# Second norm's variance from ScalarE squares, weight splitting spread over two stages, residual pieces re-timed

## The reference

```python
x = x + xattn(layernorm(x), ctx, ctx)     # per batch [512, 2048]
x = x + ffn(layernorm(x), up, down, perm)
# xattn: t = Wt@v, p = Wp@q, g = Wg@k; att = sum(p*g) per group of 64 rows
#        y = Wz @ (att*t) per group; group norm over the group; y*gn_w + gn_b + v
# ffn:   t = x[:, perm] -> 16 heads of 128 columns
#        gelu(t @ up[h]) @ down[h] per head (128 -> 512 -> 128), then the columns back by unperm
```

## Time and profile before

| | us |
|---|---|
| median of 3 runs | 1635.8 (1634.0 to 1637.0) |
| the profiled execution's own time | 1637.5 |
| its span | 1635.7 |
| TensorE busy | 1536.8 (94%) |
| VectorE busy | 1313.6 (80%) |
| ScalarE busy | 922.3 (56%) |
| GpSimd busy | 820.2 (50%) |

### The profile page before, as it was taken

One profiled execution on the slowest core, in us unless ns is written; L12 is line 12 of the kernel. 1 busy time (PEld: TensorE's weight loads), 2 busy tenths in 40 slices (PEclk: granted clock), 3 DMA queues, 4 the chain that ended last, 5 costly groups with the idle time before them and its releaser, 6 DMA issues.

```text
span 1635.7 us, 19277 instructions
## 1 busy us (share of the span) xinstructions
PE 1536.8 (94%) x6592; PEld 1236.0 (76%) x6592; DVE 1313.6 (80%) x1872; ACT 922.3 (56%) x949; POOL 820.2 (50%) x717
## 2 busy tenths in 40 slices
...
GB/s 316 360 303 353 271 236 132 334 212 249 109 243 252 255 165 155 285 210 249 146 216 276 206 266 99 247 246 263 207 129 258 231 276 136 148 144 305 208 266 203
DMA packets 127024, 374.77 MB, mean 229 GB/s; under 512 B 24528, under 2 KB 32720, under 8 KB 118736
## 3 DMA queue, kind: packets, MB, share of 16 engines
...
## 4 chain that ended last, share of the span: by engine, by line
PE 64%; DVE 18%; DMA 6%; ACT 6%; issue 5%; POOL 1%; SPq 1%; POOLq 0%; ACTq 0%; DVEq 0%
PE PP L796 17%; PE PP L850 14%; PE PP L782 14%; PE PP L835 14%; PE PP L809 5%; DVE Z L1062 3%; DVE R L1104 2%; DVE R L954 2%; DVE HX L1104 2%; DMA FB<-in_down 1%; DMA WW<-w_scratch 1%; ACT R L875 1%; DVE bn L1067 1%; DVE FB L1110 1%; DMA xg_scratch<-FB 1%
## 5 line engine op out<-in xcount | busy, mean ns | idle before, releaser
L835 PE MATMUL PP<-GG,WW 128*128 128x512 f32 x1536 | 395.5, 394 | 17.3 <-DVE GG L1099 8.6
L782 PE MATMUL PP<-R 128*128 128x512 f32 x1536 | 361.5, 395 | 16.5 <-DVE R L954 14.1
L796 PE MATMUL PP<-R,WC 128*128 128x512 f32 x1536 | 355.6, 393 | 17.6 <-ACT Z L887 16.8
L835 PEld LDWEIGHTS PP<-GG,WW 128*128 128x128 f32 x1536 | 286.9, 189 | 89.2 <-issue 25.4
L782 PEld LDWEIGHTS PP<-R 128*128 128x128 f32 x1536 | 290.9, 191 | 82.5 <-ACT R L875 10.2
L796 PEld LDWEIGHTS PP<-R,WC 128*128 128x128 f32 x1536 | 291.6, 190 | 80.5 <-ACT Z L887 17.7
L850 PE MATMUL PP<-R,WW 128*128 128x512 f32 x1050 | 275.2, 398 | 11.3 <-DVE R L1104 7.7
L917 ACT ACTIVATE R<-PP 128x1024 fp32r<-128x1024 f32 x175 | 179.9, 1028 | 174.8 <-PE PP L835 169.1
L918 ACT ACTIVATE PP<-PP 128x1024 f32<-128x1024 f32 x256 | 261.5, 1022 | 0.0
L850 PEld LDWEIGHTS PP<-R,WW 128*128 128x128 f32 x1050 | 194.9, 190 | 64.3 <-issue 22.8
...
L1172 POOL TENSOR_TENSOR FB<-FB,SMM 128x512 f32<-128x512 f32 x128 | 167.7, 1310 | 117.2 <-DVE GG L1099 81.2
...
## 6 DMA issues: line engine op xcount, KB each, us to landing
...
```

Of the source, the lines that this page charges most:

```text
L782: t = eng.matmul(s_bank(c1), l[:, part(c1)], r, start=(dt == 0 and j == 0), stop=(dt == ND - 1 and j == 2))
L796: t = eng.matmul(PP[2 + ot // 2][:, ot % 2, :], WC[:, l, ct, part(ot)], u[:, r + ct, :], start=(ct == 0 and j == 0), stop=(ct == NT - 1 an ...
L835: t = eng.matmul(PP[slot["up", f, p]][:, e, :], wt[:, l, part(2 * p + e)], g[:, r, :], start=(j == 0), stop=(j == 2))
```

## The change

It has four parts.

1. **Second norm.** `bn_x1` and `aggr_x1` go. `mean_x1` works the mean of the new x out of numbers that are there (A times y's mean, and the row sum of x + context over D). `square_x1` lets ScalarE take (x1 - mean) squared with its accumulator, 8 instructions of 128x1024 per batch; the squares themselves are thrown into PSUM banks 2 and 3 (in the last slot, into X). `sum_sq` (VectorE, 128x4) adds the halves. For batches 1 to 6 the squares stand in the first 5 units of the next slot's S, and `xln2` and the transposes (`TURN`) move later with them. Batch 0, which has its pieces in slot 1's S anyway, gets all of it some 2 to 3 units earlier.
2. **Weights.** Only heads 10 to 15, 8 and 9 are split at t = 16 to 34. Heads 2 to 7, 0 and 1 are split from t = 88.3 on, one each 2.9 units, all through the single pair FB[4:6]. The two heads split last stay in WW, so slots 1 and 2 load their first two heads no more (8 `load_w` fewer).
3. **Pieces.** The 8 `x1_piece` of a slot stand one in each pair of units from f0 + 6.97 on, just behind `add_r`; `resid` and `gather` stand behind `scatter` (lead - 0.8 and lead - 4.85, before -1.5 and -6).
4. **Statistics of X** in slots 1 and 2 stand in the S stage, ordered by X's rows. `load_x` of batch 2 moves into slot 2's S.

```diff
-TURN = [(17.9, 20.4, 23.2, 26.0)] + [(5.2, 10.0, 16.2, 21.6)] * 6
+TURN = [(15.9, 19.0, 22.3, 25.5)] + [(10.2, 15.0, 19.6, 24.2)] * 6
...
+    def raw_w(h):
+        k = 2 * (h % 2) if h > 7 else 4
+        return [("FB", k), ("FB", k + 1)]
...
-    for k in range(ND):
-        h = (k + 8) % ND
-        put(8 + 2.3 * k, load_raw, h)
-        put(11 + 2.3 * k, w_hi, h)
-        put(11.2 + 2.3 * k, w_lo, h)
-        put(12.6 + 2.3 * k, keep_w, h)
+    split = [(16 + 2 * k, h) for k, h in enumerate((10, 11, 12, 13, 14, 15, 8, 9))]
+    split += [(88.3 + 2.9 * k, h) for k, h in enumerate((2, 3, 4, 5, 6, 7, 0, 1))]
+    for t, h in split:
+        put(t, load_raw, h)
+        lag = 2.4 if h > 7 else 1.6
+        put(t + lag, w_hi, h)
+        put(t + lag + 0.2, w_lo, h)
+        put(t + lag + 1.6, keep_w, h)
...
-                t = y0 + 0.1 + q + 0.2 * ct if i == 1 else s0 + (4 * q + ct) * 0.85 + 0.9
-                t = 11.9 + 1.2 * q + 0.29 * ct if first else t
+                t = s0 + 2.2 + 3.3 * ct + 0.8 * q if i == 2 else s0 + (4 * q + ct) * 0.85 + 0.9
+                t = 11.9 + 1.2 * q + 0.29 * ct if first else s0 + 9.3 + 1.6 * ct + 0.4 * q if i == 1 else t
                 put(t, bn_x, i, ct, q)
...
+        for k in range(8):
+            ct, hf = k // 2, k % 2
+            t = f0 + 5 + 0.8 * k if first else f0 + 6.97 + (2 * (k // 2) + 0.02 * hf if i == 1 else 2 * k)
+            put(t, x1_piece, i, ct, hf)
+            put(t + 0.9 if first or last else base[i + 1] + 0.9 + 0.55 * k, square_x1, i, ct, hf)
+            if hf and not last:
+                put(base[2] + 3.3 * ct if i == 1 else t + 0.1, load_x, i + 1, ct)
+        put(f0 + (4.1 if first else 5.1), mean_x1, i)
+        e = f0 + 12 if first else f0 + 22.4 if last else base[i + 1] + 5.4
+        put(e, sum_sq, i)
...
-            put(max(lead - 6, v0 - 3 if g == 0 else v0 - 1), gather, f, b, h)
+            put(max(lead - 4.85, v0 - 3 if g == 0 else v0 - 1), gather, f, b, h)
...
-            put(lead - 1.5, resid, f, b)
+            put(lead - 0.8, resid, f, b)
...
+                eng.activation(junk, Z[:, ct, cs], ACT.Square, bias=nm1[:, 1, ct:ct + 1], scale=1.0,
+                               accum_out=sq[:, ct, hf:hf + 1]).then_inc(S["sq"], 1)
```

More of the change, by code:

```diff
@@ L304, in g_var_b, with mean_x1 @@
         order.append(("g_var_b", i))
+    def mean_x1(i):
+        free["nm1", i] = take(("nm1",))
+        t = [n.up("nm1", i, k) for k in range(2)]
+        give(t[0], ("mvy",))
+        give(t[1], ("scol",))
+        order.append(("mean_x1", i))
     def x1_piece(i, ct, hf):
@@ L313, in x1_piece, with square_x1, sum_sq @@
         order.append(("x1_piece", i, ct, hf))
-    def bn_x1(i, ct, q):
-        n.up("bn2", i, ct, q)
-        order.append(("bn_x1", i, ct, q))
-    def aggr_x1(i):
-        for ct in range(NT):
-            n.up("mv2", i, ct)
-        order.append(("aggr_x1", i))
+    def square_x1(i, ct, hf):
+        k = 2 * ct + hf
+        if k == 0:
+            free["sq", i] = take(("sq",))
+        if i < B - 1:
+            free["sqj", i, k] = take(*banks(2 + k % 2))
+        t = n.up("sq", i, ct, hf)
+        if i < B - 1:
+            give(t, *banks(2 + k % 2))
+        order.append(("square_x1", i, ct, hf))
+    def sum_sq(i):
+        free["vr", i] = take(("vr",))
+        give(n.up("vr", i), ("sq",))
+        order.append(("sum_sq", i))
     def root_x1(i):
@@ L326, in root_x1 @@
         for k in range(3):
-            n.up("rs2", i, k)
+            t = n.up("rs2", i, k)
+            if k == 0:
+                give(t, ("vr",))
         order.append(("root_x1", i))
@@ L531, in plan @@
     w_used = {}
+    kept = []
     for i in range(B):
@@ L551, in plan @@
                 put(3 + 2 * ct, load_x, i, ct)
[L552 to L554 removed]
+        put(y0 + 2, aggr_x, i)
+        put(y0 + 2.1, root_x, i)
+        late = 1.0 if i == 1 else 0
         for q, t in enumerate((s0 + 9, s0 + 11, s0 + 13, y0 + 1.5 + late)):
```

116 lines of the change are left out of this document (62 added, 54 removed).

## The result

The changed kernel takes 1698.1 us (median of 4 runs, 1696.6 to 1698.6) against 1635.4 for the kernel before (4 runs, 1634.0 to 1637.0): a ratio of 1.0382, interval 1.0364 to 1.04. It was forecast at 1588 and is 110 us above that, and above the range. Up to slot 2's S it gives 36 of the 41 us that were forecast. The terms of slot 2's S and Y, and of the FFN work behind it, missed by 17 and by 88 us.

A forecast was written before the change was run, and what follows sets the result against it. The prediction took TensorE as the bound, with some 155 us lost around it. Its terms, -30 - 11 + 9 - 15 - 2 = -49 against 1637.5 us, gave 1588 us, range 1562 to 1617.

The forecast's parts named there:

- Slots 0 and 1 up to V: Start to slot 1's V: fewer heads and statistics there win 30 us (9 in slot 0, 21 in slot 1), bounds -12 and -44.
- Slot 1's V and FFN: Slot 1's V and FFN: fewer VectorE statistics and batch 2's X moved out win 11 us, bounds -3 and -17.
- Slot 2's S and Y: Slot 2's S and Y: eight heads chained through one buffer, landing in 6 us, cost 9 us, bounds 0 and +41.
- rival 1: Slot 2's weight chain is slow: heads land in 8 us, TensorE 25 late, 1604 us in all; 17%.
- second sign of being wrong: Slot 2: the forecast is wrong if ScalarE waits for a head for more than 5 us each time.
- slack at the end of the chain: Slot 2, behind the eighth head: 5.6 us of slack before spread_sum's result is due, taken off the chain's lag.
- FFN stages of slots 2 to 6: FFN of these five slots: 3 us won in each, -15 in all, bounds 0 and -23.
- The seam and the first piece: FFN of slots 2 to 6: 2.2 us a slot won at the seam to the next slot, 0.8 at the pieces.
- second rival: GpSimd falls behind in the FFN, held 0.9 us by each piece: 2.2 us stall in six slots, 1605 us; 12%.
- ScalarE's squares: Squares of 1.02 to 1.16 us, 8 to 9 us a slot on ScalarE, cost nothing; +12 if the cover failed.
- Slot 7: Last slot: squares fall into the FFN, VectorE gains 10.9 us; 2 us won, bounds +3 and -6.
- the fourth: Slower: slot 2's chain eats all gains if heads land in over 12.2 us; 1652 us at 14.0; 4%.

The follow-up runs named there:

- e_norm: Changed kernel with gather, resid, pieces and weights as before, leaving the second norm's part and batch 2's X: 1649.6 us, ratio 1.0099.
- b_weights: Kernel before with only the weights' part of the change added: 1642.5 us, ratio 1.0039.
- d_mix10: a_gather_back with ten heads split early and six in slot 2, in steps of 3.3 units: 1639.4 us, ratio 1.0006.
- d_mix12: a_gather_back with 12 heads split early and four in slot 2, in steps of 4 units: 1622.4 us, ratio 0.9899.
- a_gather_back: Changed kernel with only gather's due time put back to lead - 6: 1621.0 us, ratio 0.9903.
- d_w_early: a_gather_back with all 16 heads split from t = 8 on, as in the kernel before: 1615.1 us, ratio 0.9851.

## Why the prediction was wrong, point by point

- **Slots 0 and 1 up to V, -30:** V1 came at 219.0, 26.4 us earlier. The sum held, its parts did not. Slot 0 gave nothing (18.4 lost before, 19.9 after, instead of -9): the chain of the earlier trace rows did not go, it moved. ScalarE's waits for heads between 58 and 116 us are shown below. Slot 1's S, Y and the V ahead of it gave 28 instead of 21, and that is in part luck: VectorE's work there fell by 20.8 us (109.6 to 88.8) and not by the 10.9 of the statistics of Z. `s_lo` went from 1498 to 1218 ns in the mean (4.5 us), and two instructions of 128x4 from 2.4 us each to 0.2 (4.5 us). So VectorE fills 86% of the stretch instead of 93%, though 97% of Y (43.58 of 44.90), without TensorE standing still for long. Y is mostly the norm's part (e_norm: 21.2 to 3.7 lost; b_weights 15.6), S the weights' part (b_weights: 12.8 to 4.1; e_norm 15.1). The waits in slot 0, before and after:

```profile
ACT WW L869 <- DMA FB<-in_down: 19.1, 5, 7.1
```

```profile
ACT WW L899 <- DMA FB<-in_down: 22.9, 6, 8.0
```

- **Slot 1's V and FFN, -11:** from V1 to the fifth slice of slot 2's S (245.4 to 334.0 before, 219.0 to 297.7 after) 9.9 us came back. Held.
- **Slot 2's S and Y, +9:** measured +26 from that slice to V2 (334.0 to 410.6 before, 297.7 to 400.6 after), inside the bounds 0 and 41 and an us beyond rival 1's 25. The step that failed is the landing: taken as 6 us because DMA was to be less full than in slots 0 and 1, measured 7.9 in the median with the longest at 12.0, at a share of 0.98. The heads came 12.6 us apart (loads issued from 284.2 to 372.4) instead of 9.7. The first rival named this mechanism and came within an us of its price, but as a chain of eight, and d_mix10 and d_mix12 show that the number of heads is not what counts: four leave 21.4 of the 26.7 us. The second sign of being wrong that I had set, ScalarE waiting over 5 us for a head, did come: four times in slot 2, up to 11.2 us. What I called slack at the end of the chain was no cover, because each head stops ScalarE by itself, with S's and Y's own steps queued behind it.
- **FFN stages of slots 2 to 6, -15:** measured +49, the step that decided. The seam and the first piece would have been won: a_gather_back loses 7.3 a slot against 8.1, though even that is 0.8 and not 3. What failed is that `gather`'s new due time had no term of its own. It stood only in the second rival, as 2.2 us a slot charged to held scatters, with "a landing must fit in" and no landing beside it; the trace of the kernel before has none of `gather` on record. 6.9 us between `gather` and `g_hi` and a median landing of 4.2 look like a fit; the tail of up to 8.6 us, behind a held scatter, does not fit, and ScalarE waits 32 times. Measured: 9.8 a slot more than before, of which TensorE's longer wait for `g_lo` is 7.2. That `resid`, `gather` and pieces depend on each other (7.3, 13.2 and 17.0 lost in the table) was in no case of mine either.
- **ScalarE's squares at nothing:** held as a place (a_gather_back and d_w_early have them and are faster than before), not in price. One takes 1107 ns and its accumulator read 187, 1.29 together; I had 1.16 as the upper end:

```profile
L942 ACT ACTIVATE PP<-Z,nm x56: 1095/1107/1120, 146.1 to 1340.5; 128x1024 f32<-128x1024 f32 x56
L942 ACT ACTIVATION_READ_ACCUMULATOR PP<-Z,nm x56: 185/187/193, 147.2 to 1341.5; 128x1 f32 x56
```

- **Slot 7, -2:** +22, `gather` again; with it back +1.
- **The rivals:** the fourth, slower by slot 2's chain alone, was the wrong mechanism for the right sign. With 4% for all that ends slower I had priced a single cause; the loss came from rivals 1 and 2 together, the second at four times its price.
